# Two kernels of one network block: fp32 convolutions against three float32r matmuls on split operands

## The reference

```
x = x + L0(groupnorm(x))      # 32 groups of one channel each
x = x + L1(groupnorm(x))
L0: LL, LH, HL, HH = haar(x);  hf = concat(LH, HL, HH)           # 64 x 64 x 96
    x1 = lrelu(conv5(lrelu(conv5(hf, w15)), w25))
    x2 = lrelu(conv3(lrelu(conv3(hf, w13)), w23))
    x3 = lrelu(conv2(lrelu(conv2(hf, w12)), w22))
    y  = three dilated 3x3 convolutions (wd1, wd2, wd3) of x1 + x2 + x3
    phf = sigmoid(conv1(y, wca)) * hf
    z  = batchnorm(conv3(concat(LL, phf), wcb));  pLL = z * sigmoid(z)
    return inverse_haar(pLL, conv1(phf, whf), HL, HH)
L1: for each pixel the nearest of 512 codebook rows of 32 numbers
```

## Time and profile before

| | |
|---|---|
| median of three runs | 2291.51 us |
| profiled execution, first to last instruction (the page gives no other time for it) | 2164.4 us |
| PE, DVE, ACT, POOL busy | 92%, 84%, 49%, 58% |
| POOL's indirect DMAs (L1053) | 1000.9 us in 1024 |
| PE's products (L542) on hf | 888.5 us in 1824 records |
| DVE's L960 and L964 | 695.3 and 704.2 us in 1024 each |

### The profile page before, as it was taken

One profiled execution on the slowest core, in us unless ns is written; L12 is line 12 of the kernel. 1 busy time (PEld: TensorE's weight loads), 2 busy tenths in 40 slices (PEclk: granted clock), 3 DMA queues, 4 the chain that ended last, 5 costly groups with the idle time before them and its releaser, 6 DMA issues. The chain is left out here.

```text
span 2164.4 us, 27115 instructions
## 1 busy us (share of the span) xinstructions
PE 1984.8 (92%) x5232; PEld 946.5 (44%) x5232; DVE 1810.3 (84%) x3979; ACT 1059.2 (49%) x2018; POOL 1252.3 (58%) x1299
## 2 busy tenths in 40 slices
PE   6999999999999999999999999999999999995653
PEld 3444455444544455444544445444544445442221
DVE  4122799988999799988999899988999889888996
ACT  5134645545555545546556454546455454543331
POOL 2001277654776377663776367673776457673876
PEclk9999999999999999999999999999999999995555
DMA  6000011111110112111111111111111011110111
GB/s 203 15 10 5 20 40 43 27 29 34 46 35 21 41 36 47 25 24 41 42 36 26 42 35 41 30 24 37 43 41 26 20 25 34 30 25 20 34 37 32
DMA packets 80459, 76.97 MB, mean 36 GB/s; under 512 B 29200, under 2 KB 62608, under 8 KB 80016
## 3 DMA queue, kind: packets, MB, share of 16 engines
q1 hardware_dynamic: 45776, 50.78, 8.3%
q0 software_dynamic: 32768, 16.84, 5.2%
q10 hardware_dynamic: 1728, 7.41, 0.9%
HBM read 41.36 MB, written 16.78 MB: 27 GB/s over the span
## 5 line engine op out<-in xcount | busy, mean ns | idle before, releaser
L1053 POOL DMA_INDIRECT vqc<-in_codebook,idx x1024 | 1000.9, 977 | 545.2 <-DVE idx L964 306.4
L542 PE MATMUL ring<-hf,w_sb 128*128 128x512 f32 x1824 | 888.5, 600 | 2.9 <-ACT hf L715 2.9
L487 PE MATMUL score<-cst,yst 98*128 98x512 f32 x1024 | 788.4, 777 | 83.8 <-DVE idx L964 54.8
L960 DVE MAX8 top<-score 128x8 f32<-128x512 f32 x1024 | 695.3, 684 | 74.7 <-PE score L487 63.8
L964 DVE FIND_INDEX8 idx<-top,score 128x8 uint32<-128x512 f32 x1024 | 704.2, 690 | 0.0
L666 ACT CAST yst<-bands 32x256 fp32r<-32x256 f32 x1024 | 411.3, 402 | 174.6 <-PE score L487 162.1
L542 PEld LDWEIGHTS ring<-hf,w_sb 128*128 128x128 f32 x1824 | 341.6, 191 | 316.9 <-issue 294.2
L487 PEld LDWEIGHTS score<-cst,yst 98*128 98x128 f32 x1024 | 204.0, 202 | 395.0 <-DVE idx L964 206.3
L542 PE MATMUL ring<-ha,w_sb 128*128 128x512 f32 x704 | 347.5, 598 | 5.1 <-DVE ha L853 4.6
L542 PE MATMUL ring<-hb,w_sb 128*128 128x512 f32 x544 | 262.6, 595 | 6.8 <-DVE hb L866 6.8
L627 ACT ACTIVATE z<-ring,prm 128x512 f32<-128x512 f32 x144 | 99.0, 688 | 273.3 <-PE ring L542 272.7
(11 more groups left out here) (101 smaller groups left out, 1276.8 us busy)
## 6 DMA issues: line engine op xcount, KB each, us to landing
xnat<-in_x SPq DMA_DIRECT2D x128, 128.0 KB, 2.7
yst<-yl SPq DMA_DIRECT2D x512, 32.0 KB
vqc<-in_codebook,idx POOLq DMA_INDIRECT x1024
out<-vqc SPq DMA_DIRECT2D x128, 128.0 KB
w_sb<-in_weights ACTq DMA_DIRECT2D x1, 1920.0 KB, 8.2
w_sb<-in_weights ACTq DMA_DIRECT2D x3, 384.0 KB, 12.8
w_sb<-in_weights ACTq DMA_DIRECT2D x1, 1152.0 KB, 15.6
w_sb<-in_weights ACTq DMA_DIRECT2D x1, 960.0 KB, 8.6
```

Source lines behind the costliest of these rows:

```text
L487: nc.tensor.matmul(score[BANK["tile", t]][:, :], yst[0:KST, j % 2, g, wp], cst[0:KST, :], start=True, stop=True).then_inc(s_tile, 1)
L542: t = nc.tensor.matmul(ring[g % RING][:, :, :], w_sb[:, SLOTS[n, m, kind, ky], :], own(source(n, m, kind), half, slice(PAD + di, PAD + di ...
L960: nc.vector.max(top8[:, t % 4, :], score[BANK["tile", t]][:, :]).then_inc(s_top, 1)
L1053: nc.gpsimd.indirect_dma_start(vqc[:, c % 2, w * CH:(w + 1) * CH], None, codebook[:, :], bass.IndirectOffsetOnAxis(idx[:, c % 2, k, 0:1], ...
```

## The change

Five things change together.

1. The convolutions that read the normalized bands (w15, w13, w12, wcb, whf; 74 of the 113 slots) take both operands split into a float32r part and a float32r remainder, and three float32r matmuls (high x high, low weights x high, high x low) in place of one fp32 product. The other 39 slots stay fp32. A round has 444 float32r and 78 fp32 products.
2. The weights no longer lie in SBUF. They are kept in DRAM as 24 pages of 8 units of 64 KB; `wring` holds four pages. SyncE's queue loads a page when the page four before it is done. In round 0 ScalarE and VectorE split the raw weights, page by page, and SyncE writes the result to DRAM.
3. The Haar sums and differences move from VectorE to GpSimd (`dwt`), with statistics left on VectorE.
4. The split inputs: ScalarE writes the high parts (`normal_own`, `normal_ll`, `weighted_high`), VectorE the low parts (`normal_low`, `ll_low`, `weighted_low`). `attend` writes its product to `br`. The edge and side copies become DMAs on SyncE's queue; ScalarE's normal_side, normal_edge and weighted_sides go.
5. `make_plan` places the other steps by the time of the products (240 ns or 870 ns each), not by their number.

```diff
+SPLIT = ("w15", "w13", "w12", "wcb", "whf")
+UNITS_PER_PAGE, NR = 8, 4
...
+MAIN, WLOW, XLOW, FULL = range(4)
+NS = {MAIN: 240, WLOW: 240, XLOW: 240, FULL: 870}
...
+        for half in range(2):
+            for terms in ((MAIN, WLOW), (XLOW,)) if part[0][0] in SPLIT else ((FULL,),):
+                steps += [("mm", n, half, m, kind, ky, term) for n, m, kind, ky in part for term in terms]
...
+MEAN2, VAR2, BIAS2, SIDES_AT, FIRST_TURN, REAR = 9000, 14000, 17000, 18000, 20000, 14000
...
-        w_sb = sb("w_sb", [P, NW, P])
+        wparts = nc.dram_tensor("wparts", [P, NP, UNITS_PER_PAGE, P], F32, kind="Internal").ap()
+        wring = sb("wring", [P, NR, UNITS_PER_PAGE, P], F32R)
...
+            def page(b, p):
+                page_freed(sp, b, p - NR)
+                n = 2 * len(PARTED[p]) + len(WHOLE[p])
+                sp.dma_start(wring[:, p % NR, 0:n, :].bitcast(F32), wparts[:, p, 0:n, :]).then_inc(s_page[p % NR], 16)
...
+                w = wring[:, p % NR, UNIT[slot, int(term == WLOW)], :]
+                t = nc.tensor.matmul(ring[g % RING][:, :, :], w.bitcast(F32) if term == FULL else w,
+                                     own(source(n, m, kind, low), half, slice(PAD + di, PAD + di + ROWS)),
...
+                        for key in group_ends(i, CONVS):                     # ScalarE, round body
+                            evacuate(b, key)
+                            if key[0] == "wca":
+                                due.append(key[1:])
+                                if len(due) > 2:
+                                    weighted_high(b, par, *due.pop(0))
...
+            def weighted_high(b, par, m, half):
+                act.wait_ge(s_q, 6 * b + 2 * m + half + 1)
+                nc.scalar.activation(own(hf[:, m, 0], half), br[m][:, half * HALF:(half + 1) * HALF, :],
+                                     ACT.Identity, bias=0.0, scale=scale1[par][:, :]).then_inc(s_ph, 1)
...
+            def normal_low(n, par, m):
+                dve.wait_ge(s_hfh, 3 * n + m + 1)
+                nc.vector.scalar_tensor_tensor(out=hf[:, m, 1, :, PAD:PAD + ROWS], in0=raw(par, BANDS[m]),
...
+            def weighted_low(b, par, m, half):
+                dve.wait_ge(s_ph, 6 * b + 2 * m + half + 1)
+                nc.vector.scalar_tensor_tensor(out=own(hf[:, m, 1], half),
...
+                        for key in group_ends(i, CONVS):                     # VectorE, round body
+                            if key[0] in LEAKY:
+                                leaky(b, *key)
...
+                            elif key[0] == "wca":
+                                weighted_low(b, par, key[1], key[2])
...
+            def dwt(n, par, k):                                              # GpSimd
+                pool.wait_ge(s_xev, XCHUNKS * n + k + 1)
+                wait(pool, s_dwt, XCHUNKS * n + k)
+                slot, js = xt[:, k % 2], slice(2 * k, 2 * k + 2)
+                pair = sd[:, :].rearrange("p s j e i -> p e j s i")
+                nc.gpsimd.tensor_tensor(sd[:, 0], slot[:, 0], slot[:, 1], ALU.add).then_inc(s_sd, 1)
+                nc.gpsimd.tensor_tensor(sd[:, 1], slot[:, 1], slot[:, 0], ALU.subtract).then_inc(s_sd, 1)
+                pool.wait_ge(s_sd, 2 * (XCHUNKS * n + k + 1))
+                nc.gpsimd.tensor_tensor(bands[par][:, 0, js], pair[:, 0], pair[:, 1], ALU.add)
+                nc.gpsimd.tensor_tensor(bands[par][:, 1, js], pair[:, 1], pair[:, 0], ALU.subtract)\
+                    .then_inc(s_dwt, 1)
+            def attend(b, par, m, half):
+                pool.wait_ge(s_free, NG * b + GROUP["wca", m, half] + 1)
+                nc.gpsimd.tensor_tensor(br[m][:, js, :], raw(par, BANDS[m])[:, js], br[m][:, js, :], ALU.mult)\
+                    .then_inc(s_q, 1)
...
-                        gather(v, t)
+                        if pending is not None:
+                            gather(v, pending)
+                        pending = t
```

More of the change, by code:

```diff
@@ L29 @@
 XTURN = 10
-LEAD, REAR = 9, 16
 BANKS = 4
@@ new lines, with make_pages @@
+UNITS = make_units()
+USED = [x for unit in UNITS for x in unit if x[0] != "cbmap"]
+assert sorted(SLOTS[x] for x in USED) == list(range(NW))
+def make_pages():
+    pages, room = [], 0
+    for x in USED:
+        size = 2 if x[0] in SPLIT else 1
+        if size > room:
+            pages.append([])
+            room = UNITS_PER_PAGE
+        pages[-1].append(x)
+        room -= size
+    return pages
+PAGES = make_pages()
+NP = len(PAGES)
+assert NP % NR == 0
+PARTED = [[x for x in page if x[0] in SPLIT] for page in PAGES]
@@ new lines, with slot_runs @@
+WHOLE = [[x for x in page if x[0] not in SPLIT] for page in PAGES]
+PAGE = {x: p for p, page in enumerate(PAGES) for x in page}
+UNIT = {}
+for _p in range(NP):
+    _n = len(PARTED[_p])
+    UNIT.update({(x, low): i + low * _n for i, x in enumerate(PARTED[_p]) for low in range(2)})
+    UNIT.update({(x, 0): 2 * _n + i for i, x in enumerate(WHOLE[_p])})
+SPLIT_PAGES = [p for p in range(NP) if PARTED[p]]
+def slot_runs(items):
+    runs = []
+    for at, x in enumerate(items):
+        if runs and SLOTS[x] == runs[-1][1] + runs[-1][2]:
+            runs[-1][2] += 1
+        else:
+            runs.append([at, SLOTS[x], 1])
+    return runs
@@ L134, with first @@
 RUN_ENDS = [x[1] for x, y in zip(TURNS, TURNS[1:] + [("end",)]) if x[0] == "tile" and y[0] not in ("tile", "ychunk")]
+MEAN2, VAR2, BIAS2, SIDES_AT, FIRST_TURN, REAR = 9000, 14000, 17000, 18000, 20000, 14000
 def make_plan():
[L140 to L167, removed]
+    plan, starts, now = [], [], 0
+    for unit in UNITS:
+        for x in [unit[0]] if unit[0][0] == "cbmap" else unit_steps(unit):
+            plan.append(x)
+            starts.append(now)
+            now += NS[x[6]] if x[0] == "mm" else 0
+    def first(ns):
+        return next(i for i, t in enumerate(starts) if t >= ns)
+    at = {}
+    for what, ns in (("mean2", MEAN2), ("var2", VAR2), ("bias2", BIAS2), ("side", SIDES_AT)):
+        at[first(ns)] = [(what,)]
+    places = [i for i in range(first(FIRST_TURN), first(now - REAR))
               if not (plan[i][1] in ("w22", "wd1", "wd2", "wd3") and plan[i][4] != OWN and plan[i][2] == 1)]
+    for i in list(places):
+        if plan[i][0] == "mm":
+            places += [i] * (NS[plan[i][6]] // 60 - 1)
+    places.sort()
     for k, x in enumerate(TURNS):
@@ L1019, in _ @@
             var1(0, 0, 1)
+            for m in range(3):
+                normal_low(0, 0, m)
             dve.wait_ge(s_const, 16 * 4)
@@ L1104, in _ @@
                 pool.sem_inc(counter, PRIMED)
-            nc.gpsimd.memset(power[:, :], -0.5)
-            tiles = [t for pair in (*hf, (lln,), side, ha, hb) for t in pair]
-            for t in tiles:
-                last = nc.gpsimd.memset(t[:, :, :], 0.0)
-            last.then_inc(s_zero, 1)
-            pool.wait_ge(s_zero, 1)
+            nc.gpsimd.memset(power[:, :], -0.5).then_inc(s_pow, 1)
+            pool.wait_ge(s_pow, 1)
+            for k in range(XCHUNKS):
+                dwt(0, 0, k)
             norm(0, 0)
```

522 lines of the change are left out of this document (354 added, 168 removed).

## The result

The changed kernel takes 2511.41 us (median of four runs, 2505.03 to 2522.45) against 2290.85 us of the kernel before in the same job (four runs, 2286.85 to 2291.81): ratio 1.098, 95% interval 1.0947 to 1.1012. It is slower, as forecast, but by 220 us, not 64, and 96 us above the upper end of the range.

What follows compares the result with a forecast made beforehand. PE (92% busy) looked like the bound, with POOL setting the long stretch after the change. 225 + 6 x 260.2 + 236.7 + 204.9 = 2227.8, plus 127.1 around the span: 2355 us, 2.8% slower; 8-in-10 range 2220 to 2415.

Steps and rivals of the forecast that it cites:

- the long stretch: First gather to first attend: from 171.7 us, set by PE, to 172, set by POOL; PE 152.7, VectorE 159.
- the attention: Six attend: POOL, ScalarE and VectorE take turns of 5.1 us; 22.5 instead of 13.8, or 21.2 start to start.
- the first round: Start to first L914: 240.1 less 23.8 of PE, plus 5 at the start and 4 at the attention, 225 us.
- The distance from the span to the median of the runs, taken as unchanged: Outside the profiled span: 2291.5 - 2164.4 = 127.1 us, added to the forecast span of 2227.8.
- Last attend to L914, 25.6 + 23.2: Round's end: to var1's power, then 19.7 plus 3.5 for three normal_low; originally 47.5 together against 42.0 before.
- All this costs nothing: Page loads hidden, asked for over 20 us ahead; ScalarE's swapped copies also free; no time added.
- PE's prices: Per product on PE: float32r 0.235 us (bounds 0.21 and 0.43), fp32 0.866; saves 23.8 a round if PE set time.
- rival (d): PE's long stretch: float32r at 0.30 in a row makes it 173, level with POOL; 2360 us; within the forecast's 0.48.
- The four Haar operations of a chunk: dwt on GpSimd: 0.68 us each, 2.7 a chunk, bounds 2.0 and 4.4.
- (a): Faster: attention waits met early, six attend 13.8, dwt 2.0 a chunk; round 244.5, total 2252 us; chance 0.22.
- (b): As (a), and POOL no bound, working ahead: stretch 159, round 236.5, total 2204 us; chance 0.1.
- (c): Heavier: dwt at upper bound (+12 a round) or PE's clock falling in stalls (+5); total 2415 us; chance 0.2.

Runs made afterwards that it cites:

- e1: The kernel before, run again with a profile and no edit; 2255.28 us, span 2253.5.
- e3: Changed kernel with weighted_low moved from the wca group ends to its first use on VectorE; 2486.98 us, ratio 1.1002.
- e8: Changed kernel with weighted_low put later, behind a search (from the fourth wca group on); 2416.10 us, ratio 1.0596.
- e9: Changed kernel with the hf edge copies moved from the end of SyncE's round to behind the next x loads; 2495.92 us, ratio 1.0927.
- e10: Changed kernel with three of GpSimd's four Haar operations of a chunk left out from the third image on; 2496.91 us, ratio 1.0948.
- e4: Changed kernel with the four Haar operations of a chunk back on VectorE; 2479.70 us, ratio 1.0962.
- e5: Changed kernel without the second float32r product (high data by low weights), 148 of 444 left out; 2541.26 us, ratio 1.1263.
- e6: Changed kernel with one fp32 product in place of each float32r triple, low parts still made and waited for; 2527.19 us, ratio 1.1177.
- e13: Kernel before with each fp32 product issued as two of 256 columns; 2328.54 us, ratio 1.0284.
- e2: Changed kernel without reloading weight pages from the second image on; 2438.11 us, ratio 1.080.
- e12: Changed kernel with each float32r product issued as two of 256 columns; 2544.03 us, ratio 1.1234.
- e7: Changed kernel with the edits of e3 and e4 together; 2476.23 us, ratio 1.0946.
- e11: Changed kernel with the edits of e8 and e9, and Haar steps shared, two on VectorE and two on GpSimd; 2387.80 us, ratio 1.0482.
- e14: Kernel before with the four Haar operations of a chunk on GpSimd, nothing else changed; 2293.15 us, ratio 1.0134.

## Why the prediction was right in sign and wrong in size

The step that failed is the sum of the long stretch, from the first gather to the first `attend`. The prediction took GpSimd's work for it, 172 us, and had no term for stops; it took 197.3, of which 19.0 were lost in stops. That is 25.3 of the 38.2 us by which each of the six rounds was missed. The ends of the round, where the pages were put at nothing, missed 3.5 and 4.6, the attention 3.6, the way to the power 1.2.

The forecast's span was 2227.8 us, measured 2506.9. The difference of 279.1: the first round 8.6 (233.6 for 225), six rounds 229.5 (1790.7 for 1561.2), the seventh 30.8, the tail 10.2. Against it stand 125.3 us added around the span that are not there (127.1 for 1.8). The two errors have opposite signs, and that the total missed by 154 us and not by 279 is luck.

- **"The distance from the span to the median of the runs, taken as unchanged"**: failed. e1's span is 89.1 us longer than the trace's, 12.1 in each of six rounds, 10.3 of them PE's stops before the 108th gather, which the trace I read did not have; what the first job's runs added to that, up to 2290, no trace here shows. A time in the rounds isn't carried over as a constant: it went from 10.9 to 19.0 us a round with the change. The hint was on the table: an own time for the profiled execution was missing.
- **The long stretch, "172, set by POOL"**: the size is near for the stretch without stops (rest 177.3 up to the 108th gather, which comes 1 us before the `attend`), and the measured 197.3 is that plus 19.0. The cause was wrong. Against e3, e8 and e9 up to the 106th gather (188.4 in the mean), taking 14 to 16 us off GpSimd gave 4.5 (e10), moving its Haar steps 2.6 (e4), a third of PE's float32r work 7.3 (e5); 23.8 us a round more of PE's cost nothing (e6, 187.3). So no one engine's sum sets it. Without what was lost the time to the 106th gather is 166 to 173 us in all kernels but e13, however much was lost, 0 to 22 us: a stop is lost in full, and the 19 us that PE had to spare covered nothing. That the order of the four programs, with at most four tiles between PE and VectorE, sets the 170 is the reading left over; no run changed the number of `score` banks.
- **The attention**: right mechanism, right rows, every link as written. 5.1 us a turn were 5.9, since VectorE's `weighted_low` waits for a `weighted_high` that started 1.31 behind its `attend`, and the gather starts 0.8 behind the search: 24.8 for 21.2. Against the kernel before it is 12.2 a round; e8 bought it back and shows it as the largest single cost, 87 us of the 220.
- **Last attend to L914, 25.6 + 23.2**: the first held (26.8), the second was 27.8. The three `normal_low` are in it, 3.68 in one timeline row, as forecast; the rest is the `side` copies behind pages, and the branch (e2: 24.0 without pages).
- **"All this costs nothing"** of the pages: failed, 41 us (e2). I had looked at whether PE waits for a page, and not at what stands behind the pages: `side`, x loads, output, and the branch.
- **PE's prices**: 26 float32r products in a row took 6.50 us, 0.25 each, for 0.235: right, so rival (d) is out. The four Haar operations of a chunk have records of 0.75 to 0.81 us in the mean, and mostly 3.05 to 3.1 us lie between the first one's start and the next gather: less the usual gap of 0.30, 2.8 for 2.7. `low`, `add` and gather are nearly as before. PE's row in the changed kernel:

```profile
1399.14 6.50 PE L808 MATMUL ring<-hf,wring 128*128 128x512 f32 x26
```

- **Rivals**: (a) and (b) are out, as the turns are there, and without them (e8) the rounds are still 283.5, not 244.5. (c) was the nearest, 2415: the clock does fall in stalls (52 times at the lower level, 51 to 65 us a round, against 1 to 16 in e1). But in the first 108 gathers of a round one takes 1.89 us at the lower level and 1.80 at the upper: a sign of the stalls, rarely their price.

What stays open is the stops' cause. They gather at certain tiles of a kernel (of the changed kernel's 44 in seven rounds 31 are near the 9th, 20th, 36th and 69th tile, others near the 53rd and 99th), though not in every round. They come in both kernels, not from pages (e2), not in step with PE's instructions (e12, e13), less with fewer products (e5). They are fewer in all three kernels that put Haar steps back on VectorE (e4, e7, e11) and more with them on GpSimd (e14), but e10 left nearly all of them. Nor do the packets by which the queues bring instructions mark them: 9 of the 44 stops overlap one, in e1 4 of 25, no more than stretches of that length taken elsewhere. Nor was it tried why one execution of the kernel before had none.

## What to carry to other kernels

Before a difference between span and measured time is carried over, ask whether it can lie around the span at all; if the trace is of a quicker execution than the timed ones, time inside the rounds is missing from it, and it scales. Where engines exchange small tiles in order, an instruction that waits for another engine goes behind the work that its own consumers need, not in front of it and not at its last possible place: the first costs a turn at each tile, the second moves the turn to the next pair (e3), one search later it costs little (e8). A stream that is early enough for its reader can still be late for whatever shares its queue: list what is behind it, and look at the loop's branch (how queued transfers hold it up, no run here shows). And where small tiles set the pace, less work on the busiest engine need not shorten a round (e5, e6).

## What the runs showed of the hardware

- The granted clock falls to the lower of its levels (1.2 of 2.4 GHz) behind stops and in the turns of the attention; in the round shown it came back after 3.4 to 10.2 us in the long stretch and after 27 in the attention. With a third of PE's float32r products left out the mean grant fell from 0.876 to 0.827.
- VectorE's instruction behind the loop's branch came 1.9 to 2.1 us late in the kernel before, and 5.8 and 6.9 us late in the changed one, with pages and edge copies (510 KB each, 10.0 us to landing) under way; 3.8 to 7.5 in the variants that kept both there. Either taken away brought it back: 1.9 and 2.1 without pages (e2), 2.4 and 2.5 with the edge copies moved (e9).
- In e8 `weighted_low` lasts 1755 ns in the mean instead of 829, 2.20 in the row shown: its record begins 0.36 us before GpSimd's `attend` of 1313.73 and ends 0.56 behind that one's end. The Trainium skill (SBUF — State Buffer, "SBUF: two separate sides") has a VectorE instruction with two SBUF inputs and a GpSimd instruction that reads SBUF exclude each other for the whole instruction; the trace agrees that one waits for the other. That the first to start goes first, which the section also has, the row does not show: VectorE's record starts first, and it waits. A gather was under way then (1312.73 to 1313.72), but a gather alone lengthens nothing: 42 Haar differences (L824) of the kernel before that overlapped only gathers took 0.42 us in the mean. It cost VectorE 44 us in the run (84.0 for 39.7 in 48), beside the 87 gained.
- By the distance between starts of weight loads a pair of 256-column products costs PE almost what one of 512 does: in e13 a half record of an fp32 product takes 0.218 us for 0.434 (medians, products on hf), in e12 a float32r one 0.123 for 0.242. Yet e13's time to the 106th gather without what was lost is 7.2 us longer than e1's; where these lie, no run shows.
